# Mixture-of-experts tail of a four-stage block: per-buffer counts for the scatter-add, and a real-tile count rounded to even

## The reference, cut to what matters

```python
x = hidden_states.reshape(-1, 512)
scores = sigmoid(x @ gate_w.T) + bias           # bias is spread widely: experts are used very unevenly
topk_w, topk_idx = top_k(scores, 4)
topk_w = topk_w / (sum(topk_w) + 1e-20)
cw = sum(one_hot(topk_idx, 16) * topk_w[..., None], axis=1)
g = einsum('th,eih->eti', x, Wg);  u = einsum('th,eih->eti', x, Wu)
zw = silu(g) * u * cw.T[:, :, None]
out = einsum('eti,ehi->th', zw, Wd)
out = out + silu(x @ Sg.T) * (x @ Su.T) @ Sd.T  # shared expert
```

## Time and profile before

| | |
|---|---|
| runs | 793.66 us median (792.67 to 798.17, 3 runs) |
| span of the profiled execution | 786.5 us |
| PE busy / weight loads | 717.1 us (91%) / 417.3 us |
| DVE / ACT / POOL busy | 324.2 / 222.4 / 191.3 us |
| scatters `out<-rq,sidx` | 37, of 1596 ns on POOL |
| gathers `rq<-z_rows,gidx` | 38, of 1003 ns on POOL |
| loads of experts' weights | 9, 1536 KB each |
| PE's clock over the span | 0.970 of full |

### The profile page before, as it was taken

One profiled execution on the slowest core, in us unless ns is written; L12 is line 12 of the kernel. 1 busy time (PEld: TensorE's weight loads), 2 busy tenths in 40 slices (PEclk: granted clock), 3 DMA queues, 4 the chain that ended last, 5 costly groups with the idle time before them and its releaser, 6 DMA issues.

```text
span 786.5 us, 9564 instructions
## 1 busy us (share of the span) xinstructions
PE 717.1 (91%) x2582; PEld 417.3 (53%) x2583; DVE 324.2 (41%) x801; ACT 222.4 (28%) x599; POOL 191.3 (24%) x271
## 2 busy tenths in 40 slices
PE   5998899989999999999999898969898988999990
PEld 3564344435778777677755654534444443454440
DVE  3686633440125656765755653751121211121220
ACT  3453232324234433333343421311121211122220
POOL 1243410110000000202202040422444443454531
PEclk9999999999999999999999989999999999999995
DMA  9700400040000000000120000086555456454441
GB/s 330 273 1 1 160 1 0 1 160 1 0 1 1 1 0 15 14 1 14 11 85 14 14 1 14 27 291 225 146 133 107 94 146 214 95 92 93 83 77 27
DMA packets 20737, 58.29 MB, mean 74 GB/s; under 512 B 3633, under 2 KB 6961, under 8 KB 19025
## 3 DMA queue, kind: packets, MB, share of 16 engines
q0 software_dynamic: 9440, 19.83, 13.2%
q1 hardware_dynamic: 9200, 34.13, 12.1%
q10 hardware_dynamic: 2064, 3.93, 1.4%
HBM read 43.43 MB, written 14.58 MB: 74 GB/s over the span
## 4 chain that ended last, share of the span: by engine, by line
PE 55%; DMA 26%; DVE 7%; issue 6%; ACT 2%; POOL 2%; POOLq 1%; ACTq 0%; DVEq 0%
PE ps L1032 25%; DMA out<-rq,sidx 22%; PE ps L1187 11%; PE ps L1023 3%; PE ps L1175 3%; PE ps L1159 3%; PE ps L1108 2%; PE ps L1109 2%; PE ps L1118 2%; DMA rq<-z_rows,gidx 2%; DVE rq L852 1%; DMA r<-in_ctxT 1%; DVE r L921 1%; ACT r L643 1%; PE ps L1055 1%
## 5 line engine op out<-in xcount | busy, mean ns | idle before, releaser
L1032 PE MATMUL ps<-kv,rq 128*128 x444 | 203.6, 608 | 0.6 <-ACT rq L690 0.5
L1032 PEld LDWEIGHTS ps<-kv,rq 128*128 128x128 f32 x444 | 83.7, 196 | 93.5 <-issue 93.3
L1032 PE MATMUL ps<-zT,r 128*128 128x256 f32 (+1 forms) x400 | 92.8, 388 | 0.6 <-ACT rq L634 0.6
L1187 PE MATMUL ps<-r 128*128 128x512 f32 x192 | 87.0, 604 | 1.0 <-DVE r L921 1.0
L1032 PEld LDWEIGHTS ps<-zT,r 128*128 128x128 f32 x400 | 75.0, 190 | 14.9 <-issue 4.3
L980 DVE TENSOR_TENSOR rq<-ps,rq 128x256 f32<-128x256 f32 x37 | 15.7, 424 | 150.6 <-ACT rq L694 150.6
L643 ACT ACTIVATE r<-ps,snm 128x128 f32<-128x128 f32 x128 | 45.3, 366 | 106.2 <-DVE snm L905 106.2
L527 POOL DMA_INDIRECT out<-rq,sidx x37 | 59.1, 1596 | 38.7 <-POOL sidx L523 26.1
L490 POOL DMA_INDIRECT slots<-tokw,sloti x32 | 32.3, 1009 | 146.6 <-DVE sloti L964 139.3
L465 POOL TENSOR_SCALAR ve<-mv 128x1 f32<-128x1 f32 x32 | 7.2, 226 | 232.1 <-DVE mv L821 232.0
L1187 PEld LDWEIGHTS ps<-r 128*128 128x128 f32 x192 | 36.2, 194 | 42.0 <-issue 40.4
(11 more groups left out here) (164 smaller groups left out, 943.7 us busy)
## 6 DMA issues: line engine op xcount, KB each, us to landing
kv<-in_experts SPq DMA_DIRECT2D x9, 1536.0 KB, 7.3
r<-in_Wq SPq DMA_DIRECT2D x1, 3072.0 KB, 9.9
r<-in_Wo SPq DMA_DIRECT2D x1, 3072.0 KB, 10.1
r<-in_ctx SPq DMA_DIRECT2D x8, 256.0 KB, 9.6
xr<-in_x SPq DMA_DIRECT2D x8, 256.0 KB, 9.4
z_rows<-zrow SPq DMA_DIRECT2D x8, 256.0 KB, 2.7
r<-in_shared SPq DMA_DIRECT2D x1, 1536.0 KB, 11.0
r<-in_V SPq DMA_DIRECT2D x1, 1376.0 KB, 11.9
```

Of the source, the lines that this page charges most:

```text
L1032: mm = pe.matmul(out, lhs(k), rhs(k), start=(k == 0), stop=(k == n - 1))
L1187: mm = pe.matmul(ps[:, 7, :], oT[:, j % 2, m, :], wo[:, m, :], start=(m == 0), stop=(m == NQT - 1))
```

## The change

- `s_ys` becomes two semaphores, one for even and one for odd tiles. `add_rows(i)` waits before the index copy only for its own buffer's last scatter, i-2, and behind the copy for a number of landings in the other one, read from a new part of `tab` (195 to 242) by `rows_before(i)`. That number stands for all landings up to i-1 where tile i is the first of its expert (or padding), and up to i-3 elsewhere. For tiles 1, 2 and 3 it is written in the code, and means all up to i-1.
- VectorE works this part out in `route_weights` from a new constant `landed`, seven operations ahead of the weights table, and two more ahead of `tab[193]` and `tab[194]`.
- The real tile count is rounded up to an even number (`odd24`); `tail` is that number less 4. The loops start at tile 4 and run in pairs, and the last tiles stand outside. The tiles worked on are `tail + 4`, and there are as many gathers.
- The index copies of gathers 0 and 1 stand ahead of both gathers, and a gather reads its column behind its waits rather than ahead of them.

```diff
-        s_ys = sem("expert_rows_added")
+        s_ys = [sem(f"expert_rows_added{i}") for i in range(2)]
...
-            def add_rows(i, par):
+            def add_rows(i, par, before):
                 col = pool.value_load(tab[0:1, bass.ds(i, 1)], min_val=0, max_val=P)
-                if not isinstance(i, int) or i:
-                    pool.wait_ge(s_ys, 16 * i)
+                if not isinstance(i, int) or i >= 2:
+                    pool.wait_ge(s_ys[par], i * 8 if par == 0 else i * 8 - 8)
                 pool.tensor_copy(sidx[:, par:par + 1], ids[:, bass.ds(col, 1)]).then_inc(s_si, 1)
+                if before is not None:
+                    pool.wait_ge(s_ys[1 - par], before)
                 pool.wait_ge(s_si, i + 1)
                 pool.wait_ge(s_yc, i + 1)
...
+            def rows_before(i):
+                return pool.value_load(tab[0:1, bass.ds(i + 195, 1)], min_val=16, max_val=8 * TILES + 16)
...
+            for i in range(4):
+                next_gather(i + 4, i % 2)
+                add_rows(i, i % 2, (None, 16, 16, 32)[i])
+            with pool.Fori(4, tail, 2) as n:
+                for i, par in ((n, 0), (n + 1, 1)):
+                    next_gather(i + 4, par)
+                    add_rows(i, par, rows_before(i))
+            for i in range(4):
+                add_rows(tail + i, i % 2, rows_before(tail + i))
...
-                link(dve.tensor_scalar(tt[:, 2, 0:24], even24, endT[:, E - 1:E], None, ALU.is_le))
+                link(dve.tensor_scalar(tt[:, 2, 0:24], odd24, endT[:, E - 1:E], None, ALU.is_le))
...
+                first = tt[:, 0, 0:47]
+                link(dve.tensor_tensor(first, tf[:, 49:96], tf[:, 48:95], ALU.subtract))
+                link(dve.tensor_scalar(slots, iota48, endT[:, E - 1:E], None, ALU.is_ge))
+                link(dve.tensor_tensor(first, first, slots[:, 1:48], ALU.max))
+                link(dve.tensor_scalar(first, first, 16.0, None, ALU.mult))
+                link(dve.tensor_copy(tf[:, 195:196], landed[:, 0:1]))
+                link(dve.tensor_tensor(tf[:, 196:243], first, landed[:, 1:48], ALU.add))
+                link(dve.tensor_copy(tab[:, 195:243], tf[:, 195:243]))
...
+            with pe.Fori(4, tail + 2, 2) as n:
+                pe_step(n, 0)
+                pe_step(n + 1, 1)
...
+            pe_step(tail + 2, 0, copied)
...
+            down(tail + 1, 1, tail, old)
+            act_in(tail + 2, 0, tail + 1)
+            gate_up(tail + 3, 1, load, at)
...
+            down(tail + 2, 0, tail + 1, old)
+            act_in(tail + 3, 1, tail + 2)
+            down(tail + 3, 1, tail + 2, at)
```

More of the change, by code:

```diff
@@ L503, in _, with index, gather @@
             pool.wait_ge(s_pad, 2 * 16)
-            def gather(i, par, wait_rows, n):
+            def index(i, par):
                 col = pool.value_load(tab[0:1, bass.ds(i, 1)], min_val=0, max_val=P)
-                if wait_rows is not None:
-                    pool.wait_ge(s_tx, wait_rows)
-                    pool.wait_ge(s_gx[par], n * 16)
                 pool.tensor_copy(gidx[:, par:par + 1], ids[:, bass.ds(col, 1)]).then_inc(s_gi, 1)
+            def gather(i, par):
                 pool.wait_ge(s_gi, i + 1)
@@ L705, in _ @@
             x_copy(0, 0)
-            for i in range(5):
+            for i in range(4):
                 act_step(i, i % 2)
-            with act.Fori(3, 2 * pairs - 2, 2) as n:
-                act_step(n + 2, 1)
-                act_step(n + 3, 0)
-            z_copy(2 * pairs, 0)
+            with act.Fori(4, tail + 2, 2) as n:
+                act_step(n, 0)
+                act_step(n + 1, 1)
+            act_step(tail + 2, 0)
+            z_copy(tail + 2, 0)
+            silu(tail + 3, 1)
+            z_copy(tail + 3, 1)
         @block.vector
@@ L994, in _ @@
             dve.wait_ge(s_ids, 1)
-            pairs = dve.value_load(tab[0:1, 193:194], min_val=16, max_val=TILES // 2)
-            for i in range(5):
+            tail = dve.value_load(tab[0:1, 194:195], min_val=28, max_val=TILES - 3)
+            for i in range(4):
                 if i >= 2:
-                    y_copy(i - 2, i % 2, i - 3 if i > 3 else None, column(i - 2))
+                    y_copy(i - 2, i % 2)
                 mul(i, i % 2)
-            with dve.Fori(3, 2 * pairs - 2, 2) as n:
-                for i, par in ((n + 2, 1), (n + 3, 0)):
-                    col = column(i - 2)
-                    y_copy(i - 2, par, n - 1 if par else n, col)
+            with dve.Fori(4, tail + 4, 2) as n:
+                for i, par in ((n, 0), (n + 1, 1)):
+                    y_copy(i - 2, par)
                     mul(i, par)
-            last = dve.value_load(tab[0:1, 194:195], min_val=30, max_val=TILES - 3)
-            for i in (1, 2):
-                col = column(last + i)
-                y_copy(last + i, i % 2, last + i - 1, col)
+            for i in (0, 1):
+                y_copy(tail + 2 + i, i)
         @block.tensor
@@ L1345 @@
     i = np.arange(P)
-    cst = np.zeros((P, 4 * P + 176), f)
+    cst = np.zeros((P, 4 * P + 224), f)
     cst[:, 0:P] = np.eye(P)
```

80 lines of the change are left out of this document (39 added, 41 removed).

## The result

| | before | after |
|---|---|---|
| runs, median | 795.91 us (792.67 to 798.87, 4 runs) | 769.38 us (768.99 to 772.41, 4 runs) |
| ratio | | 0.9694, 95% interval 0.9659 to 0.973 |
| span of the profiled execution | 786.5 us | 767.1 us |
| mark 0 | 540.42 us | 542.69 us |
| mark 0 to the end of the span | 246.1 us | 224.4 us |

The kernel is faster by 3.1%, 769.4 us against the 770.1 forecast. The change shifted lines: L514 is now L515, L523 is L531, L527 is L538, L444 is L445, L990 is L1020, L1023 is L1050, L1032 is L1059.

What follows compares the result with a forecast made beforehand. Taken as the bound: the chain of scatters on POOL keeps pace with PE, so one slow scatter stops PE. 6.3 + 4.5 + 8.3 + 0.3 + 4.2 = 23.6 us; 786.5 - 23.6 + 7.2 = 770.1 us, range 764 to 780.

Steps and rivals of the forecast that it cites:

- Number of tiles: Routed loop: 36 tiles instead of 37 spare PE one step (5.81) and four transposes (0.5), 6.3 us won.
- Load at mark 7: Expert load behind mark 7 (PE's transposes behind tile 7's down product): gathers 11, 12, 13 in time, 4.5 us won.
- rival 2: Loads at marks 7 and 15 still catch gathers 11 and 19, two stalls, together 8.6 us: 778.7 us, chance 0.24.
- Loads at marks 15 and 17: Marks 9 to 20: a stall of 3.2 us plus 1.6 slow clock stays of 13.1, 8.3 us won.
- Marks 0 to 7: First steps: the index copy leaves the path and a late gather 8 goes, the load table comes later; 0.3 us won.
- New pieces: Added VectorE operations hidden behind PE's wait for gather 1, POOL's added table read covered by PE's 5.81: 0 us.
- The end: Behind the last down product: the last scatter starts 2.0 us behind instead of 6.1, 4.2 us won.
- The rule weighed: DMA engines alternate between queues packet by packet, so gather 21 would land early (765.3 us); the sum did not use it.
- The third: The stall at gather 21, behind the load at mark 17, goes too, winning its 4.8 us: 765.3 us, chance 0.13.
- The fourth: Landings of scatters did not make gathers late; only tile and end are won: 783.2 us, chance 0.06.
- The fifth: 37 real tiles, rounded up to 38, so 5.8 - 0.5 us are spent instead of 6.3 saved: 781.7 us, chance 0.02.
- The sixth: POOL becomes the bound, its loop passing 5.81 us through the added table read: slower, 805 us at 2.0, chance 0.03.

Runs made afterwards that it cites:

- tiles_38: The kernel after with two tiles of padding added to the tile count (38 instead of 36): 785.04 us, 0.991 of the kernel before.
- start_relaxed: The kernel after, but tile 2 waits only for its own buffer and tile 3 for tile 0: 768.01 us, 0.963 of the kernel before.
- reads_early: The kernel after with both table reads of a scatter between the gather's index copy and the gather, same waits: 770.05 us, 0.967 of the kernel before.
- second profile: The kernel after, unchanged, run again beside three others: 772.5 us, 0.973 of the kernel before.
- before_copy_first: The kernel before with each scatter's index copy moved ahead of its wait, nothing else changed: 784.04 us, 0.9882 of the kernel before.
- wait_all: The kernel after, but every scatter waits for the landing of the one before, index copy ahead of the wait: 776.15 us, 0.977 of the kernel before.
- gather_first: The kernel after with the gather of tile k+5 issued ahead of the scatter of tile k: 762.33 us, 0.9625 of the kernel before; again 762.43.
- chain_36: The kernel after, but every scatter waits for the one before, index copy behind that wait: 791.35 us, 0.9964 of the kernel before.

## Why the prediction was right or wrong

**Number of tiles, -6.3: as forecast.** 36 scatters and gathers. From mark 32 to the end of the last matmul the kernel before took 20.33 us (747.44 to 767.77) and the kernel after 14.09 (738.57 to 752.66), 6.24 less. The run tiles_38 shows that an added tile costs at least its step.

**Load at mark 7, -4.5: wrong.** Marks 7 to 9 lost 4.5 before and lose 4.8 after. The step that failed is "Gather 11 starts at mark 7 - 1.2, 1.6 ahead of the load". It takes scatter 6 to be 2.0 behind its mark, as in a quiet stretch. But tiles 1 to 3 keep their waits and the early loads make them late, 5.9 us at tile 3, and POOL's own loop of 5.39 us recovers 0.4 a tile. The gather went out with the load. The outcome is rival 2's at this one place, but not for its reason: a lead of 1.6 us is free, as gather 19 shows (635.88, ahead of the load at 637.47, with no stall behind it), only gather 11 did not have it. The runs start_relaxed and reads_early each take the lateness away by another route, and with it the stall. I had POOL's loop at 5.3 and used it only to ask whether it is under 5.81, not how fast it catches up.

**Loads at marks 15 and 17, -8.3: right in place, about right in size, and credited to the wrong part.** The stall left is at mark 18, as forecast, of 1.98 us and without a slow clock, where I had 3.2 + 1.6. Marks 9 on lose 2.7 us in the first profile and 5.9 in the second, on both sides of the 4.8 forecast; the gain is 10.4 or 7.2. What won most of it was not that scatters no longer wait for each other: behind mark 9 before_copy_first, which keeps every wait, loses 3.7, and wait_all, which keeps them too, 6.6. The step that failed is "Only the index copy leaves the path (0.2 each, twice)". The price was nearly right, 0.27 us a link as measured. But I counted it in marks 0 to 7 alone and left it out of every other link. There the chain ran at PE's own pace (5.80 against 5.81), so that 0.12 us a tile is the difference between a scatter that stays late until the next load and one that gets clear of it.

**Marks 0 to 7, -0.3:** it was -1.0 (3.6 to 2.5), the far end of what I gave, and -3.4 in the second profile, outside it.

**New pieces, 0: as forecast.** Mark 0 came 2.27 us later, but the router's product (eight matmuls, ahead of everything that changed) was already 2.23 late, 489.52 against 487.29. POOL's loop is 5.39 (5.3). The second read of the table does find the queue free: 0.29 us.

**The end, -4.2: as forecast, -4.3.** 1.8 us from the last matmul's end (750.68 + 1.98) to the last scatter, and 14.4 us instead of 18.7 to the end of the span. This is what the relaxed waits themselves buy: with all waits kept the last scatter starts 5.7 us later.

**Sum and total.** From mark 0 to the end 21.7 us were won, not 23.6: marks 7 to 9 took 4.8 off, marks 9 on gave 2.1 back, marks 0 to 7 0.7 and the end 0.1. With mark 0 2.3 later, the spans differ by 19.4, 4.2 less than the sum. The time still came out within 1 us because a second term was wrong the other way: I took 7.2 us as lying around the span, from a span and a median of different executions. In the runs with a profile 1.8 to 1.9 lie around it (767.1 and 768.99 in the kernel after). So the profile of before is of an execution of about 788.4 us (an estimate, 786.5 + 1.9), some 5 us faster than the median of 793.66 that I used. 770.1 - 5.3 + 4.2 gives the 769.0 of the profiled execution. By the medians the gain is 26.5 us; no profile here shows where the 7 us lie that the two spans do not. The total being so near is luck.

**The rule weighed: the trace agrees with its turns, and I read them wrongly.** The two queues move 75 and 74 packets in the same 3 us. That is what the Trainium skill says ("DMA: Bandwidth & Descriptors", Queues, rings and completion order): each engine goes round its queues packet by packet. Its packets hold several descriptors, and whether the profile counts the same packets no run shows. I had compared times of landing only and concluded that a gather waits for the load. It takes turns with it, but each turn of the load carries six times the bytes and takes 2.8 times as long. Nor did gather 21 land early, as I had taken the rule to mean: it took 6.7 us to reach PE. How long a gather takes depends on where in the load it falls, 8.60 us with its start and 6.7 when 0.9 behind. The turns alone do not give these two figures, and why a gather issued with the load fares worst is open.

**Rivals.** The second (the loads still catch gathers 11 and 19) had one of its two stalls, for another reason, as said above. The third (the stall at gather 21 goes too) fell: it stayed, at 1.98. The fourth (landings don't make gathers late) is refuted by start_relaxed. The fifth (38 tiles) fell with the 36 scatters. The sixth (POOL the bound) fell, although POOL's loop turned out to matter as the rate of recovery.

## What to carry to other kernels

In a chain of transfers that wait for each other, look at the link, not at the wait: everything between a landing and the next issue is paid in every link (1.21 us here, 0.94 with the index copy moved out of it). Where link and consumer are equal (5.80 and 5.81) a single delay does not heal, and 0.1 us a tile decides what the next load meets. Price a moved instruction in every link that it leaves, and follow lateness tile by tile from where it arises to the next large load before calling a stall gone. Put urgent small transfers ahead of work that may be late (the gather before the scatter: 0.9625). Cutting the large loads that run beside them helped the gather that starts with a load, and little one that starts behind it; the two edits together gave 757.8 us, 0.9546 of the kernel before. And subtract a profile's span from the time of its own execution, not from a median.

## What was not expected of the hardware

- A load of 1536 KB in rows of 12 KB beside a transfer in rows of 2 KB: equal packets (75 and 74), six times the bytes. Cut into six, the load no longer delayed the gather issued 0.4 us ahead of it, but gathers 1.3 and 2.3 us behind it still took 6.2 and 7.0 us to reach PE.
- A lead decides: a scatter 1.2 us ahead of a load took 8.99 us to land, one 2.0 ahead 4.92.
- The granted clock averaged 0.81 in the 9 us from the end of a wait of 3.01 us on, and stayed at 1.00 behind one of 1.98 us. But it also stayed at 1.00 behind one of 3.10 us, in gather_first run again, so the length of the wait alone does not decide.
- The time to mark 0, ahead of every changed scatter, varied by 11 us between profiles (539.8 to 551.3). In the latest case, start_relaxed, PE waited 5.62 us for the table of slots. What delays that transfer is open.
- The landings of scatters in a quiet stretch differ from profile to profile: 4.60 us in the mean in the kernel before and 4.81 in chain_36 (scatters 9 to 13). That is three quarters of the difference between their links. Why is open.
